# Cross-attention and feed-forward on one core: blocks of four batches become unrolled pairs of two

## What is computed

```python
def attention(q, k, v, Wq, Wk, Wv, Wfc, bfc):     # 32 heads of 16, 8 key and value groups
    qh, kh, vh = heads(q @ Wq.T), heads(k @ Wk.T), heads(v @ Wv.T)
    score = einsum('bhqd,bhkd->bhqk', qh, repeat(kh, 4)) / 4
    out = einsum('bhqk,bhkd->bhqd', softmax(score), repeat(vh, 4))
    return merge(out) @ Wfc.T + bfc

def ffn(x, w_gating, w_linear):                    # 512 -> 2 x 2048 -> 512, operands in e4m3
    return qdot(gelu(qdot(x, w_gating[0])) * qdot(x, w_gating[1]), w_linear)

x = x + attention(layernorm(x), ctx, ctx, ...)
x = x + ffn(layernorm(x), ...)
```

## Time and profile before

| | us |
|---|---|
| median of three runs | 534.07 (532.03 to 534.3) |
| span of the profiled execution | 530.9 |
| TensorE busy | 456.3 |
| VectorE busy | 388.4 |
| ScalarE busy | 324.8 |
| GpSimd busy | 207.8 |

### The profile page before, as it was taken

How to read it: one execution, slowest core, us unless ns; L and a number is a source line. 1 busy time by engine, 2 the same in 40 slices (tenths; PEclk the granted TensorE clock), 3 DMA queues, 4 the chain that set the end, 5 groups by cost and what they waited for, 6 DMA issues and landing times.

```text
span 530.9 us, 9268 instructions
## 1 busy us (share of the span) xinstructions
PE 456.3 (86%) x3000; PEld 302.1 (57%) x3000; DVE 388.4 (73%) x765; ACT 324.8 (61%) x639; POOL 207.8 (39%) x196
## 2 busy tenths in 40 slices
PE   3945597679997998898997998898998979989997
PEld 2834475457854565557853555567744646656643
DVE  5945889899635878999536879999546887777541
ACT  4550265564355896883465796883475786875971
POOL 2200376675200057983300067982300076981000
PEclk9985556778999998999999998999998997999999
DMA  8899834440537301113346401114264001110002
GB/s 305 278 230 222 317 140 148 136 158 6 115 80 159 140 25 44 44 41 79 79 99 138 161 2 42 42 40 99 61 136 104 4 4 43 46 51 29 1 2 80
DMA packets 18500, 52.11 MB, mean 98 GB/s; under 512 B 3872, under 2 KB 4896, under 8 KB 16416
## 3 DMA queue, kind: packets, MB, share of 16 engines
q1 hardware_dynamic: 18464, 51.66, 34.3%
HBM read 28.05 MB, written 4.19 MB: 61 GB/s over the span
## 4 chain that ended last, share of the span: by engine, by line
issue 33%; PE 23%; POOL 17%; DVE 16%; DMA 4%; SPq 4%; ACT 2%; POOLq 0%; DVEq 0%; ACTq 0%
POOL plo L1224 12%; SPq L309 3%; PE bank L611 3%; PE bank L456 2%; PE bank L385 2%; DVE ao L1020 2%; DMA qs<-cq 2%; POOL x L1231 2%; PE bank L387 2%; PE bank L386 2%; PE bank L554 2%; PE bank L571 2%; PE bank L577 2%; PE bank L544 2%; POOL rstd L1200 2%
## 5 line engine op out<-in xcount | busy, mean ns | idle before, releaser
L1224 POOL TENSOR_TENSOR plo<-p,phi 128x512 f16<-128x512 f32 x128 | 154.1, 1226 | 194.7 <-ACT phi L762 194.5
L989 DVE TENSOR_REDUCE mx<-bank 128x4 f32<-128x512 f32 x128 | 86.5, 683 | 43.0 <-PE bank L456 41.0
L759 ACT ACTIVATE p<-bank 128x512 f32<-128x512 f32 x128 | 78.3, 612 | 29.0 <-PE bank L474 28.3
L456 PE MATMUL bank<-ks,qs 96*128 96x256 f32 x256 | 77.0, 394 | 21.9 <-DMA qs<-cq 19.6
L456 PEld LDWEIGHTS bank<-ks,qs 96*128 96x128 f32 x256 | 54.3, 232 | 42.4 <-issue 13.0
L762 ACT ACTIVATE phi<-bank 128x512 f16<-128x512 f32 x128 | 78.2, 611 | 0.0
L474 PE MATMUL bank<-qs,ks 100*128 100x512 f32 x128 | 67.3, 526 | 2.8 <-ACT phi L762 1.3
L794 ACT CAST ff<-bank 128x512 bf16<-128x512 f32 (+3 forms) x71 | 38.8, 546 | 32.3 <-PE bank L554 30.6
L600 PE MATMUL bank<-wlin,act 128*128 128x512 fp8e4 x192 | 56.9, 400 | 0.0
L489 PE MATMUL bank<-vt,plo 128*128 128x49 bf16 x512 | 48.3, 195 | 2.9 <-POOL plo L1224 2.2
L554 PE MATMUL bank<-x2T,wgate 128*128 128x512 fp8e4 x192 | 50.5, 386 | 0.0
(11 more groups left out here) (104 smaller groups left out, 837.7 us busy)
## 6 DMA issues: line engine op xcount, KB each, us to landing
stage<-in_w SPq DMA_DIRECT2D x24, 512.0 KB, 3.9
qs<-cq SPq DMA_DIRECT2D x48, 256.0 KB, 5.0
ks<-khl SPq DMA_DIRECT2D x48, 128.0 KB, 2.4
xin<-in_x SPq DMA_DIRECT2D x16, 256.0 KB, 5.5
cin<-in_ctx SPq DMA_DIRECT2D x4, 1024.0 KB, 5.0
x<-in_x SPq DMA_DIRECT2D x16, 256.0 KB, 2.8
out<-x SPq DMA_DIRECT2D x16, 256.0 KB, 2.0
x<-in_w SPq DMA_DIRECT2D x5, 512.0 KB, 6.9
```

Source lines behind the costliest of these rows:

```text
L456: mm = pe.matmul(A[(n + 1) % 2][:, 2 * SEQ * j:2 * SEQ * (j + 1)], qs[0:SROWS, pair, j0 + j, tok(i)], ks[0:SROWS, pair, :, tok(i)], start= ...
L759: act.activation(p32[:, n % PBUF, :], T[n % 2][:, :], ACT.Exp, scale=QUARTER).then_inc(p32_ok, 1)
L989: dve.tensor_reduce(mx[:, i % 2, :, pair, j0:j0 + 2].rearrange("p a j -> p j a"), A[(n + 1) % 2][:, :].rearrange("p (j a k) -> p j a k", j ...
L1224: pool.tensor_tensor(plo[:, n % PBUF, :], p32[:, n % PBUF, :], phi[:, n % PBUF, :], ALU.subtract).then_inc(plo_ok, 1)
```

## The change

`NB` becomes 2, and the four blocks become eight pairs, all written out: there is no loop left. For pair `p` and its neighbour `q = p + 1` the order is:

- **Softmax stage of `p`**: 16 slots and four more. In them lie the second projection of pair `p - 1` (two matmuls in every slot), and by the tables `S_K`, `S_V`, `S_X`, `S_Q` (method `prepare`) keys, values, transposed x and queries of `q`: keys in slot 1, values in 2 and 3, x in 4 and 5, queries in 6 to 9. For `q = 1`, which is prepared beside pair 0, these are slots 5 to 13.
- **Feed-forward stage of `p`**: eight units (`up`), each of 16 + 16 fp8 matmuls of 128 columns: one batch of tokens and four pieces of the hidden dimension share a bank, in place of four batches and one piece. In each unit lie two score steps of `q`, all sixteen in all. The context of pair `p + 2` is split in the units 5 to 7.

Projections of keys and queries now have 256 moving columns, and the moves to `ks` and `qs` half the bytes each; `ks`, `qs` and `vt` have two copies. All banks of the first kind (`A`) are taken in one written sequence (`bank_sequence`). Further parts: the maxima are negated in the reduction itself (`negate=True`), so that `negated` falls away and two rows are moved, not four; the second norm writes fp8 and is turned by fp8 matmuls (`ident8`); the second projection is added from its bank, without the bf16 copy `y`; and x stays in a ring of three buffers and is loaded once. Of the fp8 weight chunks, fifteen are clamped on GpSimd (`chunk_clamp`) and cast on ScalarE (`chunk_cast`), nine stay on VectorE (`chunk`, one in each of the slots 0 to 8 of pair 0). ScalarE loads the exp table explicitly after each feed-forward stage (`exp_table`) and the GELU table in slot 15.

The core of the diff:

```diff
-NB = 4
+NB = 2
...
+S_SCORES = {True: {0: 2, 1: 2, 2: 2, 3: 2}, False: {}}
+S_MAX = {True: 5, False: 0}
+S_K = {True: 5, False: 1}
+S_V = {True: (6, 7), False: (2, 3)}
+S_X = {True: (8, 9), False: (4, 5)}
+S_Q = {True: (10, 11, 12, 13), False: (6, 7, 8, 9)}
+S_NORM = {True: 4, False: 0}
+TURN_OUT, PROJECT_OUT, RESIDUAL, TURN_X2 = 11, (12, 13), 14, 17
+DOWN = [(0, 1, 3), (0, 3, 5), (0, 5, 7), (0, 7, 9), (0, 9, 11), (0, 11, 13), (0, 13, 15), (0, 15, 16)]
+FINISH = (9, 17)
...
+            stack_max(0, 0)
+            for c in range(14, 16):
+                load_chunk(c)
+            stack_max(0, 1)
+            for c in range(16, 21):
+                load_chunk(c)
...
+            def up(p, k, part):
+
+                i, v = divmod(k, UPB)
+                u = UNITS * p + k
+                out = up_bank[k % 2][part]
...
+                for h in range(UH):
+                    for kk in range(KT):
+                        mm = pe.matmul(out[:, h * SEQ:(h + 1) * SEQ], wgate8[:, UH * v + h, kk, part, :], x2T[:, i, kk, :],
+                                       start=kk == 0, stop=kk == KT - 1)
...
+            def prepare(q, n):
+
+                first = q == 1
+                if n == S_K[first]:
+                    project_k(q)
+                for b in range(NB):
+                    if n == S_V[first][b]:
+                        project_v(q, b)
+                for i in range(NB):
+                    if n == S_X[first][i]:
+                        turn_x(q, i)
                 for j in range(HPG):
-                    project_q(t, j)
...
+                    if p and n < TILES:
+                        r_i, g = divmod(n, GROUPS)
+                        lo, hi = 2 * g, 2 * g + 2
+                        down(p - 1, r_i, lo, hi)
...
+                for k in range(UNITS):
+                    up(p, k, 0)
+                    if q < NP:
+                        if k == UNITS // 2:
+                            turn_max(q, 0)
+                        scores(q, *divmod(2 * k, GROUPS))
...
-            def negated(t, i):
...
+                                  AX_X, ALU.max, negate=True).then_inc(max_ok, 1)
...
+            def finish(r, i):
+                x1 = xr[:, r % RING, i, :]
+                dve.wait_ge(lin_done, NB * r + i + 1)
+                dve.tensor_tensor(x1, x1, G[i][:, :], ALU.add).then_inc(out_ok, 1)
```

More of the change, by code:

```diff
@@ L371, in _ @@
[L371 to L373 removed]
+            load_chunk(W_FIRST_LOADS)
+            stack_k(0)
+            load_ctx(1)
+            stack_q(0)
+            for c in range(W_FIRST_LOADS + 1, 14):
+                load_chunk(c)
+            stack_max(0, 0)
+            for c in range(14, 16):
+                load_chunk(c)
+            stack_max(0, 1)
+            for c in range(16, 21):
+                load_chunk(c)
@@ L646, in step @@
+            project_k(0)
+            for b in range(NB):
+                project_v(0, b)
+            for j in range(HPG):
+                project_q(0, j)
+            for s in range(GROUPS):
+                scores(0, 0, s)
+            turn_max(0, 0)
+            for p in range(NP):
+                first, q = p == 0, p + 1
+                n_scores = 0
                 for n in range(SLOTS):
-                    i, g = divmod(n, GROUPS)
                     if n < TILES:
-                        scores_t(t, n)
```

1613 lines of the change are left out of this document (724 added, 889 removed).

## The result

The changed kernel takes 573.37 us (median of four runs, 571.08 to 577.23) where the kernel before takes 534.18 beside it: ratio 1.071, 95% interval 1.064 to 1.078. It is slower by 7%; 532 was forecast, with a range of 507 to 565.

What follows compares the result with a forecast made beforehand. It took the kernel as bound by TensorE and VectorE in softmax, with engines idle in the 22.0 us stage and thin ends. 41 + 82 + 6 x 58.4 + 56 = 529, plus 3.2, gave 532 us, range 507 to 565.

Steps and rivals of the forecast that it cites:

- First slot at 41: Start of the kernel: first softmax slot at 41 us instead of 58.7, through halved query work and moves.
- less 5 for half the norms, context and the second batch's scores: Within the start: 5 us off the first slot for work no longer ahead of it.
- Pair 0, softmax stage 54: First pair's softmax stage: 54 us, with VectorE held 5 to 6 us each by late chunks 16 and 21.
- Pair 0, feed-forward stage 28: First pair's feed-forward stage: 28 instead of 24.8 us, as seven chunks land, are clamped and cast through two places.
- A middle pair of 58.4: Each of six middle pairs: 33.6 us softmax stage plus 24.8 us feed-forward stage.
- The walked waits: TensorE's waits in a middle pair, found by walking the order: 5.2 us softmax, 3.1 feed-forward, 0.4 of it hidden.
- the 2.4 at the end: End of a middle pair's softmax stage: TensorE waits 2.4 us for the second norm.
- the score pair: Feed-forward stage: two score matmuls take 0.24 us, sixteen such pairs 3.8 us.
- Up matmuls at 0.056: Feed-forward stage: 128-column fp8 up matmuls cost 0.056 us each, 256 of them 14.3 us a pair.
- The rival by which weight loads bound them: Up projections: weight loads set 128-column matmuls at 0.078 us each, adding 45 us, for 577; chance 0.06.
- Last pair 56: Last pair, without preparation of another: 26 to the first up matmul, 19, 6.9 and 3.9; 56 us.
- The slower rival: Longer pair waits with GpSimd beside VectorE and a starved first pair: 61.5 us a pair, 555 in all; chance 0.18.

Runs made afterwards that it cites:

- e1: Changed kernel with GpSimd, VectorE and ScalarE work ahead of the first slot reordered; 566.07 us, ratio to the kernel before 1.060.
- e2: Changed kernel with weight chunks 16 to 21 loaded ahead of the move of pair 0's second-batch maxima; 560.70 us, ratio 1.048.
- e14: e12 with pair 0's chunks 22 and 23 loaded ahead of key and query moves, and pair 2's context ahead of the last five chunks; 516.09 us.
- e11: e5 with the second norm's root ahead of slot 13's low weights and its application ahead of slot 15's sums; 537.80 us.
- e8: e5 with two score pairs of the next pair put ahead of the turn of the normed x; 530.02 us.
- e10: e5 with the second batch's second projection in slots 10 to 17 and its last addition in slot 19; 527.93 us.
- e12: e10 with the last addition of the pair before in slot 18 instead of 19; 522.41 us.
- e3: Changed kernel with batch 0's output projection all in slot 12 and its second norm one slot earlier; 566.73 us, ratio 1.061.
- e5: Changed kernel with four edits: start order, chunks ahead of maxima's move, batch 0's norm earlier, turned maxima's bank emptied earlier; 530.83 us, ratio 0.994.
- e9: e5 with each feed-forward unit's two score pairs together behind its second up run; 543.08 us.

## Why the prediction was wrong

- **First slot at 41 instead of 51.7: the failing step of the start.** The halved query moves held (7.48 for 6.8). What failed is the "less 5 for half the norms, context and the second batch's scores": no engine's order was walked there. The casts and the residue of pair 1's context on ScalarE and VectorE, and bias and clamps on GpSimd, stood ahead of work that the first slot needs: 8.1 us by e1. What stays after it, 43.6 for 41, was not tried.
- **Pair 0, softmax stage 54:** right (55.3), and by the mechanism named, as e2 shows. That it is so close is in part luck: the two holds were 7.3 and 7.7 us, not 5 to 6 each.
- **Pair 0, feed-forward stage 28 instead of 33.6.** The step named clamp, cast and landing of seven chunks as its pace. The clamp is 1.04 us, below the bounds given (1.37 to twice that). The pace was SP's queue: the first of these chunks is issued at 109.07, behind pair 1's query moves, which start at 101.15 and take 7.9 us. In e14, with two chunks and a context moved ahead, the stage takes 28.4. The same reason had been used for chunks 16 and 21 a few lines earlier, and not for 22 to 28.
- **A middle pair of 58.4 instead of 62.2.** The walked waits were right in their sum (7.9 for 7.6 to 8.5), the 2.4 at the end among them (1.23 + 0.98 + 0.35). Some of that is luck: the start has 0.3 for 0.9 and the first query 0.8 for 0.3, and the row from which the norm's chain was priced has TensorE at work up to the turn, so it only bounds the chain. Three prices failed: the score pair (0.24, from a row with fp32 matmuls on one side; 0.33 between fp8 ones), the end of the last matmul at each wait (not in the sum), and the clock, which the prediction had at full speed in all middle pairs. Its rows showed 1.00 and 0.97 for before, whose stages end half as often. The end of the matmul is the largest of the three, and the one that is argued and not shown.
- **Up matmuls at 0.056:** right, 16 in 0.87 (0.054 each). The rival by which weight loads bound them is refuted: the loads last 0.101 on average and are overlapped. So is, for this kernel, the 81 ns that the Trainium skill gives (TensorE: Matmul & The Clock Gate, section Back-to-back issue gap).
- **Last pair 56:** right, 55.5.
- **The slower rival** had the direction (555) and the first pair's starvation, but its mechanism, VectorE next to GpSimd, carries little: the norm's application takes 1.36 there, once a pair, and e11, which runs it ahead of the sums, only moves the wait. Its 61.5 us a pair is near the measured 62.2 for other reasons.

The sum was thus 40 us short: 8 by the order at the start and 3 more there that stay open, 6 by SP's queue late in pair 0, and 23 by three prices in the middle pairs.

## What to carry to other kernels

Walking an order gives its waits well; but a wait may cost more than the idle time that a profile lists (here 0.16 us each, an estimate). Look also at what the granted clock does behind a sparse stretch, since a stage that is cut in two has all of its waits twice. When loads are moved past a queue, check every later load in that queue, not only the first that is missed. And before moving work to cover a wait, ask what it covers where it lies: e8 and e11 only moved the wait, and e10 did until e12 moved its follower too.

## What the runs showed of the hardware

- TensorE's granted clock fell from 1.00 to 0.50 in a stretch in which it was busy for about 1 of 3 us, although no single idle stretch was longer than 1.23 us; 16 unneeded matmuls there kept it in all six middle pairs and shortened them by 0.6 us each. With the same busy time it fell in some pairs and not in others, by the profiles: with 0.97 of 3.00 in four of six in the changed kernel, in six in e1 and in five in e2; with 1.05 in three in e3 and in none in e5.
- A score pair between runs of 128-column fp8 matmuls takes 0.33: its second fp32 matmul starts 0.20 behind the first (222.04 and 222.24 in e9), the ones after it 0.12 to 0.13 behind each other.
- A GpSimd clamp of 128x1024 fp32 takes 1.04 us (median of 15), less than its 512-column operation with two inputs (1.19 on average). The norm's application on VectorE takes 0.54 to 1.36, and 1.36 at 234.66, where GpSimd works beside it.
